# Score rows 192 apart with exponentials of 384 columns, and the woven end of the second attention

## What is computed

```python
h = _L0_tok_ref(x, ...)                                  # top 179 of 256 tokens
h = h + _L0_attn_ref(_layernorm(h), ...)
h = h + _L0_ffn_ref(_layernorm(h), ...)
h = h + _L1_attn_ref(_layernorm(h), ...)
h = h + _L1_ffn_ref(_layernorm(h), ...)                  # idx = argmax(t @ Wg.T + bg)

def _L0_attn_ref(hidden_states, ...):                    # 12 heads of 16
    q, k, v = ...
    score = jnp.einsum('bhtsd,d->bhts', jnp.tanh(q[:, :, :, None, :] + k[:, :, None, :, :]), ws) + bs[0]
    p_attn = jax.nn.softmax(score, axis=-1)
    attn = jnp.einsum('bhts,bhsd->bhtd', p_attn, v)
    return attn.transpose(0, 2, 1, 3).reshape(B, T, E) @ Wo.T + bo
```

## Time and profile before

| what | us |
| --- | --- |
| median of three runs (lowest, highest) | 1369.91 (1367.65, 1370.68) |
| the profiled execution | 1369.98 |
| its span | 1368.3 |
| first tanh starts | 77.3 |
| last tanh of the first attention ends | 826.9 |
| second attention, last residual | 1262.1 |
| first transposition of the experts | 1286.5 |
| last expert tile's work on PE ends | 1359.6 |

### The profile page before, as it was taken

How to read it: one execution, slowest core, us unless ns; L and a number is a source line. 1 busy time by engine, 2 the same in 40 slices (tenths; PEclk the granted TensorE clock), 3 DMA queues, 4 the chain that set the end, 5 groups by cost and what they waited for, 6 DMA issues and landing times. The chain is left out here.

```text
span 1368.3 us, 39019 instructions
## 1 busy us (share of the span) xinstructions
PE 1124.2 (82%) x16182; PEld 858.3 (63%) x16182; DVE 1103.9 (81%) x2126; ACT 1000.6 (73%) x921; POOL 862.9 (63%) x962
## 2 busy tenths in 40 slices
PE   3767888888788778778887877985999999998496
PEld 2544655565565556555655656883667777776496
DVE  8878999999999999999999994887567777777343
ACT  0479999999999999999999995773434444442242
POOL 4088898888888888988888897654011322234254
PEclk9889999999999999999999999997999999999698
DMA  9999999100000000000000001100000200001352
GB/s 248 359 358 359 354 345 334 46 3 2 2 2 2 3 1 2 2 2 2 2 2 2 2 2 47 24 0 1 1 2 2 64 18 18 19 16 43 107 157 57
DMA packets 75451, 103.09 MB, mean 75 GB/s; under 512 B 6303, under 2 KB 73640, under 8 KB 75282
## 3 DMA queue, kind: packets, MB, share of 16 engines
q1 hardware_dynamic: 63784, 87.90, 19.6%
q10 hardware_dynamic: 6860, 6.12, 1.7%
q0 software_dynamic: 4640, 6.65, 1.5%
HBM read 18.32 MB, written 83.85 MB: 75 GB/s over the span
## 5 line engine op out<-in xcount | busy, mean ns | idle before, releaser
L932 ACT ACTIVATE work<-work 128x2864 f32<-128x2864 f32 (+1 forms) x272 | 691.7, 2613 | 11.5 <-DVE work L444 10.7
L444 POOL TENSOR_TENSOR work<-shared 128x1253 f32<-128x1253 f32 (+1 forms) x272 | 613.8, 2266 | 129.5 <-PE psum L1866 95.0
L1866 PE MATMUL psum<-work,ws_place 128*32 128x179 f32 x8640 | 396.3, 323 | 148.4 <-ACT work L932 146.4
L444 DVE TENSOR_TENSOR work<-psum,shared 128x1611 f32<-128x1611 f32 (+3 forms) x288 | 488.1, 1722 | 0.8
L1866 PEld LDWEIGHTS psum<-work,ws_place 128*32 128x32 f32 x8640 | 257.7, 111 | 256.8 <-ACT work L932 203.1
L2060 PE MATMUL psum<-shared 32*64 32x179 f32 (+1 forms) x1728 | 129.4, 341 | 1.3 <-DVE peaks L1568 1.0
L921 ACT ACTIVATE pt_region<-psum,bs_neg 128x512 f32<-128x512 f32 x144 | 100.8, 701 | 3.4 <-PE psum L1879 3.4
L2060 PEld LDWEIGHTS psum<-shared 32*64 32x64 f32 (+1 forms) x1728 | 75.2, 147 | 40.5 <-issue 27.1
L1290 DVE SCALAR_TENSOR_TENSOR p_sb<-psum,bs_col,s_top 128x358 f32<-128x358 f32 x144 | 82.2, 571 | 15.4 <-PE psum L1879 0.7
L1879 PE MATMUL psum<-ident,p_sb 128*128 128x128 f32 x544 | 92.2, 290 | 0.0
L816 POOL DMA_INDIRECT xs_dram<-w_store,slot_i x24 | 26.5, 1105 | 93.8 <-DVE slot_i L1668 83.2
(11 more groups left out here) (384 smaller groups left out, 1974.3 us busy)
## 6 DMA issues: line engine op xcount, KB each, us to landing
xs_dram<-pad_row SPq DMA_DIRECT2D x23, 3088.0 KB, 27.5
pt_region<-xs_dram ACTq DMA_DIRECT2D x19, 193.0 KB
pt_region<-xs_dram SPq DMA_DIRECT2D x19, 193.0 KB, 2.4
xs_dram<-pad_row SPq DMA_DIRECT2D x1, 2895.0 KB, 27.2
work<-in_x SPq DMA_DIRECT2D x2, 768.0 KB, 10.4
work<-in_x ACTq DMA_DIRECT2D x2, 768.0 KB, 16.3
work<-in_L_ffn_W2T SPq DMA_DIRECT2D x1, 1536.0 KB
work<-in_L_ffn_W1T SPq DMA_DIRECT2D x1, 1536.0 KB
```

What stands on the lines that cost most here:

```text
L444: ins = eng.tensor_tensor(dst[:, a * KEEP:e * KEEP].rearrange("p (u s) -> p u s", s=KEEP), k[:, h * KP:h * KP + KEEP].unsqueeze(1).to_broa ...
L932: act.activation(a, a, ACT.Tanh).then_inc(tanh_done, 1)
L1866: ins = pe.matmul(bank_s[p % 2][32 * quad:32 * quad + 32, at:at + KEEP], ws_place[:, j, :], arg_slot(n)[:, u * KEEP:(u + 1) * KEEP], start ...
```

## The change

Two edits are made together.

**The first attention.** Rows of `p_sb` stand 192 apart (ROW). The 384 columns of a duo are then three pieces of 128, where there were four of which two held 51 keys each. A middle piece holds keys 128 to 178 of the first group in its first 64 rows and keys 0 to 63 of the second group in its last 64. `turn_duo` does 3 transposes for 4, `exps` takes 384 columns for 512 (the ninth duo stays at 2 and 256), and `pt` is laid out as (piece, duo, column). For groups of odd number v has to stand at other rows: `v_extra` holds v shifted by 64 rows, and `spread_v` makes it by three small DMAs a batch (64, 64 and 51 rows of 1536 bytes), from POOL's queue within groups 4, 6 and 8 for batches 0 to 4, from SP's queue behind the fills for batches 5 to 15. PE's `context` waits for them (`v_moves`). `context` treats even and odd groups apart: 32 matmuls of 96 columns after group 5 and 32 of 48 after group 7, where 16 of 180 and 16 of 92 stood; the loop over j is now the outer one, and its two key parts stand next to each other. The bias of the pads becomes 128x384 twice (L1122), and POOL clears `v_extra` (two memsets of 128x768) ahead of `pad_row`.

**The end of the second attention.** `norm_beside(b, r)` on DVE works out the norm's numbers of batch b with the steps of `choose(r)` and `place(r - 1)` between its steps. `norm_beside(14, 12)` takes the place of POOL's `pair_norms` for batch 14 and of `route(12)`; `norm4(14)` now stands ahead of `route(13)`; `norm_beside(15, 14)` takes the place of `last_norm` and of a part of `route(14)`; then `norm4(15)`, `place(14)`, `choose(15)`, `place(15)`. PE does `prefix_mm(14)` ahead of `gate_turn(15)`, with `warm_up(4)` between, `warm_up(3)` behind `gate_mm(15)`, and, once all scatters have landed, `warm_up(8)` ahead of the experts (each a bf16 product of 128x512 whose result nobody reads). ACT stages the residuals one step earlier. POOL clears one more half of the staging ring. Some semaphores are merged.

```diff
-                dve.scalar_tensor_tensor(p_sb[p % 2][:, 0:w * KEEP].rearrange("p (a s) -> p a s", s=KEEP), s, bs_col[:, :],
+                dve.scalar_tensor_tensor(p_sb[p % 2][:, 0:w * ROW].rearrange("p (a s) -> p a s", s=ROW)[:, :, 0:KEEP], s, bs_col[:, :],
...
-                act.activation(pt[b % 2][:, :, 256 * k:256 * k + 128 * w],
-                               bank_pt[p % 2].rearrange("p (s c) -> p s c", s=2)[:, :, 0:128 * w],
+                act.activation(pt[b % 2][:, 0:w + 1, k, :],
+                               bank_pt[p % 2][:, 0:128 * (w + 1)].rearrange("p (s c) -> p s c", c=128),
...
+        def spread_v(eng, b, piece):
+
+            n, v = b % 2, v_sb[b % 2]
+            if piece == 0:
+                eng.wait_ge(v_ready, b + 1)
+                done, count = v_moves(b)
+                need(eng, done, count - 48)
+            dst, src = ((v_extra[n][HALF_K:128, 0, :, :], v[0:HALF_K, 0, :, :]),
+                        (v_extra[n][0:HALF_K, 1, :, :], v[HALF_K:128, 0, :, :]),
+                        (v_extra[n][HALF_K:LAST_K, 1, :, :], v[0:TB, 1, :, :]))[piece]
+            eng.dma_start(dst, src).then_inc(v_moves(b)[0], 16)
...
+            for b in range(EARLY, B):
+                for piece in range(3):
+                    spread_v(sp, b, piece)
...
+                    if b < EARLY and g in (4, 6, 8):
+                        spread_v(pool, b, (g - 4) // 2)
...
-                for a in range(duo(k)):
-                    for s in range(2):
-                        ins = pe.transpose(bank[:, 256 * s + 128 * a:256 * s + 128 * a + 128],
-                                           src[:, a * KEEP + 128 * s:a * KEEP + 128 * s + 128], ident[:, :])
+                for s in range(duo(k) + 1):
+                    ins = pe.transpose(bank[:, 128 * s:128 * s + 128], src[:, 128 * s:128 * s + 128], ident[:, :])
...
-                for lo, hi, c, at in spans:
-                    for s, tile in ((0, first), (1, second)):
+                for at, c, groups in spans:
+                    for odd, (lo, hi, shift) in enumerate(groups):
                         for j in range(4):
-                            ins = pe.matmul(bank_out[32 * j:32 * j + 32, at:at + 4 * (hi - lo)].rearrange("p (i c) -> p i c", c=4),
-                                            v_sb[b % 2][:, s, 4 * r + j, :], tile[:, lo:hi, c + 4 * j:c + 4 * j + 4],
-                                            start=(s == 0), stop=(s == 1))
+                            cols = bank_out[32 * j:32 * j + 32, at + shift:at + shift + 32 * (hi - lo)].rearrange(
+                                "p (k i c) -> p k i c", i=8, c=4)[:, :, 0:4, :]
+                            for step, (v, key) in enumerate(parts[odd]):
+                                ins = pe.matmul(cols, v[:, 4 * r + j, :], key[:, lo:hi, :, c + 4 * j:c + 4 * j + 4],
+                                                start=(step == 0), stop=(step == 1))
...
-            route(TAIL)
+            norm_beside(B - 2, B - 4)
             ctx1_divide(B - 1)
-            route(B - 3)
             norm4(B - 2)
+            route(B - 3)
             add_out1(B - 1)
-            last_norm()
+            norm_beside(B - 1, B - 2)
             norm4(B - 1)
-            for b in range(B - 2, B + 1):
-                route(b)
+            move_places(B - 2)
+            place(B - 2)
+            move_logits(B - 1)
+            choose(B - 1)
+            move_places(B - 1)
+            place(B - 1)
...
             prefix_mm(B - 3)
+            prefix_mm(B - 2)
+            warm_up(4)
             gate_turn(B - 1)
             gate_mm(B - 1)
-            prefix_mm(B - 2)
+            warm_up(3)
             prefix_mm(B - 1)
+            for n in range(RING):
+                pe.wait_ge(sent[n], 32 * B // RING)
+            warm_up(8)
```

164 lines of the change are left out of this document (114 added, 50 removed).

## The result

The changed kernel took **1356.68 us** (median of four runs, 1351.0 to 1357.9) beside 1370.3 us (1367.65 to 1371.65) for the kernel before: a ratio of 0.9906, 95% interval 0.9887 to 0.9925, or 13.6 us less. The forecast was 1354.5 us, so it is 2.2 us off, with the right sign and inside the range. The profiled execution took 1355.62 us (span 1353.8) for 1369.98.

A forecast was written before the change was run, and what follows sets the result against it. ACT was taken to bound the first attention (83 to 827 us), with no engine full at the second attention's end. Terms -13.2 + 0.5 + 0.8 + 0.5 + 0.4 - 4.5 = -15.5 took 1369.98 to 1354.5 us, range 1350.5 to 1364.5.

The forecast's parts named there:

- exponentials of 384 columns: First attention, ACT: 128 exponentials of 384 instead of 512 columns, 0.10 to 0.11 us less each, -13.2 us (12.8 to 14.1).
- context and DVE's reserve: First attention, PE: four column groups still run together, context 0 to +1.0 us against a 1.06 us reserve; +0.5 us in all.
- copies of v issued by POOL: First attention, batch 0: POOL, already late, issues three DMA copies and overruns its reserve by 0.5 to 1.5 us; +0.8 us once.
- ends of the first attention: Batch 15's context and ctx2 stand on the path ahead of the feed-forward products, longer by 0 to 1.4 and 0 to 0.7; +0.5 us.
- bias over 128x384: Ahead of the first tanh, DVE adds the bias over 128x384 twice for 128x77 twice; +0.4 us.
- woven end: End of second attention: norms woven into DVE's routing bring the first expert transposition 4.5 us earlier (3 to 6).
- a few tenths: Experts: the part of the end's 4.5 us gain expected from experts that start at the full clock.
- for a few batches at the edge: First attention: reason given for +0.5 us, a longer context passing DVE's reserve and costing ACT time in some batches.
- three issues of 1 us: Batch 0, POOL: copy issues priced like a scatter (0.98 to 1.08 us), two groups apart, overrunning the reserve by 0.5 to 1.5 us.
- Rival 4: First attention: copies stand behind several fills, batches 1 to 5 wait 6 us each, 1385 us in all; chance 0.02.

## Why the prediction was nearly right, point by point

| term | predicted us | measured us |
| --- | --- | --- |
| exponentials of 384 columns | -13.2 (12.8 to 14.1) | -13.5 |
| context and DVE's reserve | +0.5 | 0 |
| copies of v issued by POOL | +0.8 (0 to 1.5) | +0.24 to 0.26 |
| ends of the first attention | +0.5 | 0 (-0.1) |
| bias over 128x384 | +0.4 | +0.3 |
| woven end | -4.5 (3 to 6) | -4.5 |
| the longer steps: PE's pauses (4.2), PE at half clock once (0.9) | none | +5.2 |
| before's four steps of 47.3 us (PE at half clock) | none | -1.9 |
| rest before the first tanh | none | +0.7 |
| second attention up to the statistics of 14 | none | -1.4 |
| experts | "a few tenths" | +0.3 |

**The exponentials.** Right: 0.11 us each. Five of them stand ahead of the last tanh of batch 0 (0.55 us), 120 in the 15 steps from batch to batch (0.86 us a step, 12.9), and the other three behind the last tanh's start, where they gave no more than the 0.1 us of "ends" in the table. Of the two ways to read the price, the durations (0.11 us) were nearer than the steps (0.10).

**The context.** Right where it chose. The array reaches past three waiting records as it had past one. By the prediction's reading of the Trainium skill, TensorE: Matmul & The Clock Gate, Part 3, "The mechanism", whose rule is that matmuls start and end in program order, this run would have taken 2.6 us; this case's trace has 1.32 us in both orders. The starts aren't strictly in program order either, as the end of the run in batch 9 shows:

```profile
515.16 0.32 PE L1956 MATMUL psum<-work,ws_place 128*32 128x179 f32 x1
515.17 0.25 PE L1987 MATMUL psum<-pt_region 128*32 128x96 f32 x1
```

The first record of the scores starts 0.01 us ahead of the context's last. So for these float32 records the measurement speaks against the rule. DVE's reserve at group 13, 1.06 us by my working, was 0.92 in the mean outside batches 2 and 3, and no tanh waited there for the context. The +0.5 "for a few batches at the edge" was caution with no row behind it.

**The copies of v.** The step that failed is the bound "three issues of 1 us", taken from a scatter. POOL's timeline in batch 0:

```profile
88.63 0.85 POOL L499 DMA_DIRECT2D pt_region<-v_sb  x1
...
93.99 0.54 POOL L499 DMA_DIRECT2D pt_region<-v_sb  x1
```

The first took 0.85 us, the others 0.53 to 0.62. ACT's first wait for POOL in batch 0 stayed what it was (0.85 us for 0.84 in the earlier trace rows), but POOL's reserve ran out twice more, at groups 5 and 7, where the tanh started 0.09 us behind POOL's sum, as it had at the group it waits for. These waits are too short to be shown in brackets. They are in the time of six tanh in a row, 15.25 us for 14.99 in the earlier trace rows; with all copies on SP (paced fills) it is 14.99 again:

```profile
84.19 14.99 ACT L968 ACTIVATE work<-work 128x2864 f32<-128x2864 f32 x6 [0.85 <-POOL work L446]
```

So the copies cost 0.26 us by the tanh and 0.24 by the length of batch 0 (43.23 us for 42.99). Rival 4 didn't come: under the fills the copies by POOL landed in 5.8 to 7.7 us, and in 2.0 us behind them.

**The ends of the stage.** From the end of the last tanh to the first FFN product 6.34 us, for 6.46. Since the context wasn't longer, there was nothing to add, and the shorter last turn shows.

**Ahead of the first tanh.** The bias took 0.73 us for 0.41, as worked out:

```profile
36.27 0.73 DVE L1159 TENSOR_SCALAR p_sb<-p_sb,bs_col 128x384 f32<-128x384 f32 x2
```

but the first tanh came 1.1 us later. In its trace a run of products ends 0.4 us later (at 63.1 us), and PE's clock rises later during the products that follow, at 74.4 us for 72.7, which is another 0.7 us. Over all the kernels the first tanh started between 75.9 and 80.0 us with no order that an edit explains; why the clock rises when it does stays open.

**The woven end.** Right as a sum and in its steps. The 10.3 us won ahead of it added back, norm4(14) stood at 1255.9 (predicted: about 1256), the last slot at 1272.0 (predicted 1271.4 to 1272.9), and the last scatter ended at 1275.4 (1274.1 to 1276; the gain that goes with these bounds is 3.9 to 5.8 us, not 5.4). The clause "a few tenths of it from experts that start at the full clock" was wrong: the clock was low, and the experts took 0.3 us longer.

**What was not in the sum.** Above all PE's pauses and a stretch in which nothing was changed, -1.4 us. In that stretch PE's clock differs. The windows around the entry of the feed-forward stage, before and then after (PE's clock is the first column behind the five engines'):

```profile
848.00:853.00 5.00, 5.00 (x30) 4.95 (x30) 0.00 (x0) 2.67 (x6) 3.62 (x20) 0.71 0.71 225
```

```profile
839.00:844.00 5.00, 5.00 (x41) 4.94 (x40) 1.22 (x3) 4.04 (x8) 3.77 (x19) 1.00 0.71 225
```

At the same point of the program PE does 41 matmuls in 5 us for 30. Over the kernels of this study that stage took 414.4 to 417.6 us, with and without the edits, so I put it down to chance and not to the change.

The attention's own sum, by the 15 steps from batch to batch: 15 x 0.86 less, 1.9 less for before's four steps of 47.3 us, which are gone, 5.2 more for the longer steps: -9.6, and the steps add up to -9.6. Batch 0 gave 0.3 us, its five exponentials less the copies. So the forecast of -11.4 for the attention missed by 1.4 us only because three errors cancelled: the pauses had no term, before's longer steps had none either, and some 1.5 of 1.8 us of caution weren't needed. That the clock spared the changed kernel those four steps and gave it one is luck. With the 0.7 us before the first tanh and the 1.4 given by chance it came out within 1 us of the two spans' difference, and 2.2 us from the median. The mechanism of each of the two edits was as predicted; the largest error of the sum, PE's pauses in the 5.2 us, was hidden by others.

## What to carry to other kernels

Before adding short instructions to an engine, look at what the DMA queues are doing then: the fills, which nobody needs soon, cost nothing here while PE's code arrived in time, and about 4 us once it didn't, so spread such transfers out (5.4 us between the medians here for three lines, 3.3 of them seen in the attention). A term of a sum should have a row: three that stood for caution came to 1.8 us, of which 0.3 was there. A long step isn't one cause by its looks: look at PE's clock in it before calling it a pause. Products that keep the clock up gave 1.4 us (one trace against one) when they ran without a gap until the real work arrived; stopping 1.95 us short gave nothing.

## What the hardware showed that I had not expected

- PE stood idle for 0.3 to 2.8 us at a time in the middle of runs of matmuls without a wait while 3 MB fills kept the DMA engines full. Held back to 300 us, the fills took the pauses with them; with gaps between the fills no pause was longer than 0.9 us (2.0 to 2.3 the longest in five of the six traces with fills in one go), and with 64 more records a batch they grew to 15.3. All 48 pauses ended 1.1 to 1.6 us behind the landing of a 16 KB packet of the instruction queue.
- 64 float32 records of 96 columns, four of one column group in a row, took 1.33 us from first to last start, 1.26 in the interleaved order; 64 of 48 columns took 0.75 and 0.66, 12 and 10 ns each.
- A plain DMA issue cost POOL 0.53 to 0.85 us, a scatter 0.98 to 1.08.
- PE's clock fell to 0.50 for a few us in single batches with the same work as the others. Where that met the ninth duo's transposes, an exponential waited 0.26 to 0.38 us and the batch took 0.4 to 0.9 us longer.
- The full clock, held by 38 products, was gone within 1 to 2 us of work after an idle stretch of 1.95 us (1.00, 0.88, then 0.50), and was kept where 50 products ran on without a gap.
